# Layer 1 of a gated two-layer network: the maximum row ahead of the ring loads, and maxima two packs behind the scores

## What is computed

```
xn = layernorm(x);  x = x + attention(xn) * silu(ffn(xn))        # layer 0, then layer 1
```

```
q, k: 32 heads of 8 channels;  v: 16 heads of 16
attn = softmax(q k^T / sqrt(8) + causal)                 # 32 maps of 512 x 512 per sequence
attn = attn[even heads] - lam * attn[odd heads];  out = attn v
out  = rmsnorm(out) * g * (1 - LAMBDA_INIT);  return out @ Wo.T
ffn:  a shared expert, and the 2 best of 8 experts per token
```

## Time and profile before

| | us |
|---|---|
| median of 3 runs | 2398.45 (2398.11 to 2403.45) |
| the profiled execution, its own time | 2391.47 |
| its span in the trace | 2383.8 |
| TensorE matmuls, busy | 2139.9 (90%) |
| TensorE weight loads, busy | 1452.0 (61%) |
| VectorE, busy | 1387.2 (58%) |
| ScalarE, busy | 897.5 (38%) |
| GpSimd, busy | 689.3 (29%) |

### The profile page before, as it was taken

The page is one execution under the profiler, slowest core; times in us unless marked ns, Lnnn a source line. Parts: engine busy times, 40 slices in busy tenths (PEclk is TensorE's granted clock), DMA queues, the critical chain, the costliest instruction groups (busy, mean ns, idle before and its releaser), DMA issues. The chain is left out here.

```text
span 2383.8 us, 34344 instructions
## 1 busy us (share of the span) xinstructions
PE 2139.9 (90%) x12379; PEld 1452.0 (61%) x12476; DVE 1387.2 (58%) x2721; ACT 897.5 (38%) x1760; POOL 689.3 (29%) x852
## 2 busy tenths in 40 slices
PE   2389998999989899899989999899998999989998
PEld 1257556575656666575565756667566665657556
DVE  3465665656655665656647556566665566565664
ACT  2142451425423353434515245142542335243451
POOL 2332331313312332323314134132332233232331
PEclk7589999999999999999999999899998999999999
DMA  6823423243321533125232342224331153312523
GB/s 201 286 58 105 136 63 102 71 146 103 99 52 54 179 96 90 53 67 178 71 95 69 124 119 81 69 71 152 106 102 41 54 181 94 90 53 66 176 73 94
DMA packets 108378, 245.65 MB, mean 103 GB/s; under 512 B 17284, under 2 KB 28052, under 8 KB 108012
## 3 DMA queue, kind: packets, MB, share of 16 engines
q1 hardware_dynamic: 94012, 199.96, 27.6%
q0 software_dynamic: 14256, 43.94, 6.4%
HBM read 183.24 MB, written 59.79 MB: 102 GB/s over the span
## 5 line engine op out<-in xcount | busy, mean ns | idle before, releaser
L671 DVE TENSOR_REDUCE nmax<-bank 128x1 f32<-128x512 f32 (+3 forms) x1067 | 659.0, 640 | 396.0 <-PE bank L409 383.6
L356 PE MATMUL bank<-xnT,upring 128*128 128x512 f32 (+1 forms) x2220 | 629.7, 406 | 23.9 <-DMA upring<-up_img 23.2
L582 ACT ACTIVATE probs<-bank 128x512 f32<-128x512 f32 (+1 forms) x864 | 469.1, 559 | 369.1 <-PE bank L432 356.6
L432 PE MATMUL bank<-qring,kring 128*128 128x512 f32 (+1 forms) x1056 | 483.9, 461 | 68.8 <-PEq L1413 25.3
L405 PE MATMUL bank<-kring,qring 127*128 127x512 f32 (+3 forms) x1552 | 472.0, 357 | 49.8 <-DMA kring<-k_img 48.3
L356 PEld LDWEIGHTS bank<-xnT,upring 128*128 128x128 f32 x2220 | 400.2, 193 | 105.9 <-issue 32.3
L405 PEld LDWEIGHTS bank<-kring,qring 127*128 127x128 f32 x1552 | 277.7, 196 | 125.8 <-DMA kring<-k_img 51.6
L507 PE MATMUL bank<-wdown,hbuf 128*128 128x256 f32 x1408 | 336.3, 388 | 0.0
L432 PEld LDWEIGHTS bank<-qring,kring 128*128 128x128 f32 x1056 | 209.1, 199 | 202.9 <-ACT probs L582 98.1
L1397 POOL TENSOR_SCALAR_AFFINE_SELECT probs<-probs 128x512 f32<-128x512 f32 x256 | 162.5, 635 | 510.1 <-ACT probs L582 507.6
L507 PEld LDWEIGHTS bank<-wdown,hbuf 128*128 128x128 f32 x1408 | 264.0, 194 | 33.6 <-issue 1.7
(11 more groups left out here) (119 smaller groups left out, 1568.7 us busy)
## 6 DMA issues: line engine op xcount, KB each, us to landing
upring<-up_img SPq DMA_DIRECT2D x179, 512.0 KB, 4.1
q_img<-probs SPq DMA_DIRECT2D x102, 256.0 KB, 4.0
qring<-q_img SPq DMA_DIRECT2D x256, 64.0 KB, 1.9
kring<-k_img SPq DMA_DIRECT2D x64, 256.0 KB, 3.0
qring<-q_img SPq DMA_DIRECT2D x35, 384.0 KB, 4.8
k_img<-probs SPq DMA_DIRECT2D x48, 256.0 KB, 4.5
up_img<-hbuf POOLq DMA_DIRECT2D x22, 512.0 KB, 4.8
gring<-gate_img POOLq DMA_DIRECT2D x32, 256.0 KB, 3.7
```

The lines of the kernel that those rows point to most:

```text
L356: last = nc.tensor.matmul(out_ap, part_a(a, pa, k), part_b(b, pb, k), start=(n == 0), stop=(n == len(steps) - 1))
L432: nc.tensor.matmul(SC[n % 2][:, 0:heads * w].rearrange("p (g n) -> p g n", g=heads), kring[l][:, ks, kt * P:(kt + 1) * P], qring[l][:, s, ...
L582: nc.scalar.activation(pr, pr if biased else scores, ACT.Exp, scale=scale).then_inc(s_exp, 1)
L671: nc.vector.tensor_reduce(nmax[:, u % 2, g0:g0 + heads, qt], MX[n % 2][:, 0:heads * w].rearrange("p (g n) -> p g n", g=heads), AX.X, ALU.m ...
```

## The change

In layer 1 SyncE issues the row of unit u + 1 first and waits until it has landed; then it issues the ring of unit u + 2, without a wait for the scores, and the up load last. On TensorE the max packs run `MAX_LAG * layer_of(u)` packs behind the score packs, that is 0 in layer 0 and 2 in layer 1: score packs 0 and 1 alone, score pack 2, the wait for the ring of unit u + 1, max pack 0, score pack 3, max pack 1, and so on; max packs 9 and 10 come behind the last score pack and ahead of `pe_pv(u, 1)`. In layer 0 the wait for the ring comes after score pack 0 and no longer before it. Nothing changes on the other engines.

```diff
+MAX_LAG = 2
@@ sync, rest_of_unit(u)
                         j = TILE_AFTER[u]
+                        if not last_of_layer(u):
+                            max_row(sp, u + 1)
+                            sp.wait_ge(s_mrow[1], 16 * (u + 1))
+                        if not last_of_layer(u) and not last_of_layer(u + 1):
+                            ring_load(sp, u + 2)
                         if j + 2 < J_ALL:
                             up_load(sp, j + 2)
-                        if not last_of_layer(u) and not last_of_layer(u + 1):
-                            sp.wait_ge(s_sc, PACKS * (u + 1))
-                            ring_load(sp, u + 2)
-                        if not last_of_layer(u):
-                            max_row(sp, u + 1)
@@ tensor, unit(u)
                         more = not last_of_layer(u)
-                        if more:
-                            wait_ring(pe, u + 1)
+                        lag = MAX_LAG * layer_of(u)
                         for i in range(PACKS):
                             pe_score_pack(pe, u, i)
-                            if more:
-                                pe_max_pack(pe, u + 1, i)
+                            if more and i == lag:
+                                wait_ring(pe, u + 1)
+                            if more and i >= lag:
+                                pe_max_pack(pe, u + 1, i - lag)
                             if more and u in TILE_IN:
                                 pe_up_between(pe, TILE_IN[u], i)
...
+                        for i in range(PACKS - lag, PACKS):
+                            if more:
+                                pe_max_pack(pe, u + 1, i)
                         pe_pv(pe, u, 1)
                         if more:
                             pe_max_turn(pe, u + 1)
```

## The result

The changed kernel takes 2610.79 us (median of 3, 2605.57 to 2612.42) against 2398.45: a ratio of 1.0878, 95% interval 1.0849 to 1.0906. That is 212 us slower; 2597 was forecast, within 2470 to 2670. Its profiled span is 2606.6 us, 222.8 more than before (before's profiled execution lay 7 us under its median), and the mean granted clock went from 0.958 to 0.943.

The account below looks back on a forecast made before the run. TensorE, matmul-busy 90% of the span, was taken as the bound. Row -12, reduction chain +161, unit 4 +11 and clock +39 summed to +199 us, forecasting 2597 us against 2398.45, range 2470 to 2670.

Parts of the forecast that it names:

- The row goes first, -12: Layer 1 unit starts: the maximum row lands before the first score pack, so all 16 stalls go, -12.0 us.
- The ring late by 2.0: Layer 1, units 5 to 10: TensorE's first max pack waits about 2.0 us for the kring load, 48 times.
- The estimate by the fit: The 256 KB kring load: 2.6 us from 2.0 us plus bytes over 436 GB/s; the sum took 3.0.
- The chain of eleven, 3.35 a unit: VectorE's eleven reductions in units 5 to 10: first starts 3.15 later, plus 0.2 for normalising; 48 x 3.35 = +161 us.
- list of signs: What would show it right, including the maxima's turn at P + 12.6 in units 5 to 10 (P: first score pack's start).
- the lag's 1.2 and the stall's 2.0 are both in that: Units 5 to 10: VectorE's first reduction comes 3.15 us later, which already contains both the lag and the ring stall.
- Unit 4, +11: Layer 1's unit 4, ring loaded in the front stage: lag 1.2 plus normalising 0.2, 8 x 1.4 = +11 us.
- the 0.2 for the normalising: VectorE's normalising behind the fifth maximum, no longer beside the first tile's weighting: 0.2 us a unit, bounds 0 and 0.6.
- The clock, +39: TensorE in layer 1: half of 48 ring stalls drop the clock, 1.62 us each, +39 us; bounds 0 and 78.
- The edge read from the earlier trace: Last front tile's up-weight waits: full pace after 1.55 to 1.77 us, slow matmuls behind the shortest of 1.88 and over.
- just past that edge: The new ring stall on TensorE, about 2.0 us with some 0.6 idle before it, was placed just beyond the clock-drop threshold.
- The slow landings, in the high end only: Two slow landings per batch, 4.0 to 4.5 us, hit the ring instead of the row: 16 x 1.3, high bound only.

Follow-up runs that it names:

- the early normalising: Kernel before's SyncE order with the changed kernel's two-pack lag, and VectorE normalising behind the third maximum instead of the fifth: 2449.71 us, ratio 1.0210.
- lag 0, 2 and 4: The changed kernel with MAX_LAG set to 0, left at 2, or set to 4: 2633.87, 2610.79 and 2581.39 us.

## Why the prediction was right

**The row goes first, -12.** Right: 12.0 us of waits became 0.9.

**The ring late by 2.0.** Right in place and number of times: 48 new waits at the first max pack, 1.90 us at the mean. The k load was issued at turn + 4.18 (277.96 against the turn at 273.78), forecast 4.23. It isn't one size, though: the 32 ordinary stalls are 1.35 to 2.04, 1.55 at the mean, since the k load lands in 2.8 and not 3.0 and a stall is counted from the third score pack's end; the two of units 5 and 8 are 2.2 to 3.0. The estimate by the fit in "DMA: Bandwidth & Descriptors" in the Trainium skill, section "Anatomy of one DMA", 2.6 us for this load, is a little low; the measured 2.8 lies between it and the 3.0 of the rows.

**The chain of eleven, 3.35 a unit.** The step held: an ordinary unit at full clock takes 16.6 where it took 13.2, so 3.4. Its parts are off by 0.2 each way, and that they cancel is luck. In unit 7 VectorE's first reduction starts at 299.54, P + 3.78 (forecast P + 3.97), and the turn comes 9.02 behind it (forecast 8.62 + 0.2), so at P + 12.80. The prediction's list of signs says P + 12.6, which leaves its own 0.2 out:

```profile
299.54 1.29 DVE L672 TENSOR_REDUCE nmax<-bank 128x1 f32<-128x512 f32 x2 [3.71 <-PE bank L410]
```

The normalising costs 0.4 and not 0.2; the early normalising showed that this term is its own. That "the lag's 1.2 and the stall's 2.0 are both in that" is shown by lag 0, 2 and 4: waits for the ring of 3.2, 1.9 and 0.5 us at the mean, and ordinary units of some 16.1 (estimated), 16.6 and 16.4.

**Unit 4, +11.** Measured 5 in the profiled run. From P to the turn it grew from 9.4 to 10.4 us in every batch, 1.0 and not 1.4, 8 us in all: the 0.2 for the normalising doesn't belong there, since unit 4 is the layer's first and normalises nothing. Row to row it grew by only 5, since the time ahead of P differs between the two executions: in the fifth batch the unit took 18.0 before and 16.4 after.

**The clock, +39.** Right in kind, low in size: 35 falls at 1.5 us each, which best fits the units' lengths, are about 51 us, and filling the stall took 51 us off the same 48 units (41 off the median time). The edge read from the earlier trace rows, between 1.77 and 1.88 us, doesn't carry over. Among the 32 ordinary stalls 14 have a fall in their unit, and their length doesn't sort them: there is one at 1.40 us and none at 1.64 to 1.66. Of units 5 and 8 three have none, behind stalls of 2.17 to 2.50. What decides in a single unit is not shown. So the step "just past that edge" gave no ground for half the stalls: that 27 of 48 units had a fall, near the half that was taken, is luck.

**The slow landings, in the high end only.** This is the one term that I left out of the sum and that came. The two transitions per batch that stalled for the row before now stall longer for the ring: 2.6 at the mean where others have 1.55, since the row's landing (2.6 to 3.5 instead of 1.8) holds up the issue of the ring. By the units' lengths that is 0.9 each, 15 us, where the bound had priced 16 x 1.3 = 21.

Added up for the profiled run, from the lengths of the units: -13 for the row's stalls, 48 x 3.4 = +164 for the chain, +5 in unit 4, +15 for the late rows and +51 for the clock are 222 of the 223. The forecast's +199 misses by the clock (12 too little), the late rows (15 left out) and unit 4 (6 too much).

## What to carry to other kernels

When a wait of a few tenths is cured by putting a small transfer first and waiting for it, count what the next transfer loses: here the k load was issued 4.0 us later against the turn (turn + 0.14 became turn + 4.18), against 0.6 of slack. Ask of a "lag" what chain it delays, not only what it hides: eleven reductions have to follow the first one, so hiding the late load behind other work (lag 4) returned little more than the clock's part. And an idle of 1.4 to 2 us amid dense matmuls was followed in 14 of 32 units by a fall of the clock that cost about as much again, so that filling the stalls gained 41 us even with useless work.

## What the runs showed of the hardware that was not expected

Three rows of every batch land late in the changed kernel, those of units 5, 8 and 11: 2.4 to 3.5 us, where the other 32 rows of units 6 to 10 take 1.80 to 1.82. (That of unit 11 holds up no ring.) Units 5 and 8 are also the two of the kernel before and of the run with the row on ScalarE's queue, with 3.2 to 4.6 us against 2.4 to 3.0. In the changed kernel they coincide with a packet of the instruction queue; the table of DMA queues for the stretch from 309 to 312 us (queue: packets, MB, share), with the row's landing:

```profile
q8 instruction: 1, 0.02, 2.5%
q1 hardware_dynamic: 32, 0.01, 1.4%
...
qring<-mneg SPq DMA_DIRECT2D x1, 8.0 KB, 2.7
```

and for 292 to 295 us, without such a packet:

```profile
q1 hardware_dynamic: 32, 0.01, 1.4%
...
qring<-mneg SPq DMA_DIRECT2D x1, 8.0 KB, 1.8
```

This holds throughout: all 24 late rows have one such packet of 16 KB, which starts 0.4 to 1.5 us behind the row's issue, and none of the 32 fast ones has one in flight. The run with the filled stalls moved them without meaning to. There the packet starts 1.5 to 2.1 us ahead of the issue of unit 8's row, and that row lands in 1.8 us in all eight batches; the packet that falls within the landing is that of unit 9's row, which takes 2.6 to 3.0. So the late landings go with the packets and not with the unit. Where SyncE didn't wait for the row, it was the issue of the q loads right behind it that took longer in units 5 and 8 (2.5 to 3.2 us instead of 1.9). It isn't the whole story in the kernel before: the row of unit 8 has a packet in all eight batches, but that of unit 5 in two only, and it is late in all. That the packet causes the delay was not tried by an experiment of its own. Nor was a third ring slot, which would let the ring go far ahead of the row.
